# Softmax denominators from a column of ones in the value operand, with the masked scores and the exponentials sharing one double buffer

## The chip, the cores and the metric

The kernel runs on one core of one Trainium2 chip. The time is the device time of one execution in microseconds; lower is better. The core has five engines with queues of their own: PE (matmuls and weight loads), ACT (ScalarE), DVE (VectorE), POOL (GpSimd) and SP (which only starts DMAs here). Each works through its instructions in the order written, and they wait for each other through semaphores.

## The reference

For each of 32 samples (256 rows, width 384, with a 256 x 256 adjacency matrix) two graph layers are followed by a masked attention with 12 heads of width 32. The part that the change touches is the attention:

```python
scores = jnp.einsum('bhqd,bhkd->bhqk', q, k) / jnp.sqrt(32.)
scores = scores + beta * adj_e
scores = jnp.where(adj_e > 0, scores, -9e15)
probs  = jax.nn.softmax(scores, axis=-1)
out    = jnp.einsum('bhqk,bhkd->bhqd', probs, v)
x      = layernorm(x + out)
```

The graph layers ahead of it compute a softmax of h h^T times the adjacency, mix three projections of h with it, and normalise. The two layers are called a and b below.

## The kernel before

The kernel is a software pipeline over samples. In one turn of the loop, sample t is in layer a, sample t-1 in layer b, sample t-2 in the attention (stage c), and sample t-3 in the last norm and the store (stage d). The order of the steps on each engine is written out by hand in four lists, one for each of PE, ACT, DVE and POOL. A step is a word such as `scores.6`: the part of the step `scores` for head 6 that this engine does. The change leaves these lists alone. A turn with all stages takes 72.8 us.

For each head h of the attention the work goes like this; every `[P, 2, ...]` buffer is used by the parity of h:

- PE, `scores.h`: two matmuls into `bank_s`, of which there is one. It waits until DVE has read the scores of head h-1 (`s_msk`).
- DVE, `scores.h` (L852): two instructions, one for each half of the rows, that subtract the scaled scores from the bias and take the row minimum (`hmin`), into `masked`. There is one `masked` buffer, so DVE waits until ACT has read head h-1 out of it (`s_prob`).
- ACT, `scores.h` (L647): two exponentials from `masked` into `prob`, with the sum over the row taken by the instruction's accumulator into `hsum`. `prob` is double, so ACT waits until PE has transposed head h-2 (`s_pt`).
- PE, `weights.h` (L501): four transposes of `prob` into `bank_p`. It waits for the exponentials and for DVE's `weights.(h-1)`.
- ACT, `weights.h` (L654): `bank_p` to `pT_hi` (f16). DVE, `weights.h` (L858): the remainder, to `pT_lo`.
- PE, `attend.h`: eight matmuls into `bank_o`, with the high and low parts of the probabilities as weights and three or two bf16 parts of the values (`v_parts`) as the moving operand.
- DVE, `attend.h` for odd h (L868): sums the parts of two heads out of `bank_o`.

After the last head, DVE takes the reciprocal of `hsum` (`c_sum`, L876) and POOL multiplies and adds the residual (L997, L1001).

Between these steps stand the graph layers' steps. Those that the text comes to are `a_proj.0` to `a_proj.5` (ten matmuls each on PE; ACT copies the high part `hlrh`, L596, and DVE writes the remainder `hlrl`, L754; PE's `a_proj.3` waits until DVE has done `a_proj.1`, since both use the second `bank_w`), `a_turn` (PE transposes into `bank_u`, L440; DVE writes `attTl`, L759; POOL then masks four times, L956), and `b_resid`, `b_norm2`, `b_out` on DVE (L808, L811, L817 to L824), which end with `y_in`, the input of PE's `turn_y.0` (L388).

The written order on the two engines around heads 4 to 7 is

```python
# pe
... scores.6 a_proj.2 attend.3 a_turn.0 weights.4 scores.7 a_proj.3 weights.5 attend.4 scores.8 weights.6 ...
# dve
... weights.3 scores.6 a_proj.1 attend.3 weights.4 a_turn.0 scores.7 weights.5 b_resid.0 attend.4 scores.8 ...
```

Of the kernel before, what the change touches and what calls it, by code (L numbers as in the profile page):

```python
# [31 lines left out]
VP = 3  # L32
SLOTS = 3
# [59 lines left out]
def graph_attention_kernel(nc, x, adj, wl, ws, wr, bl, bs, br, ln_w, ln_b,  # L93
# [15 lines left out]
    with ExitStack() as ctx:  # L109
# [49 lines left out]
        v_parts = sb("v_parts", [P, NT, NH, VP, HD], BF16)  # L159
        v_rest = sb("v_rest", [P, NT, D])  # L160
        neg_adj = v_rest[:, :, 0:S]
        masked = sb("masked", [P, NT, S])
# [4 lines left out]
        att = result[:, :, :].rearrange("p i (h d) -> p i h d", h=NH)  # L167

        negmax = sb("negmax", [P, NT])
        ubias = sb("ubias", [P, NT])  # L170
        zsum = sb("zsum", [P, NT])
        ssum = sb("ssum", [P, NT])
        diag = sb("diag", [P, NT])
        inv_s = {k: sb(f"inv_s_{k}", [P, NT]) for k in "ab"}
        hmin = sb("hmin", [P, NT, NH])
        hsum = sb("hsum", [P, NT, NH])
# [4 lines left out]
        var = {k: sb(f"var_{k}", [P, NT]) for k in "ab"}  # L181
        var.update({k: mv[k][:, :, 1] for k in "yc"})
        eps = {"a": EPS_GRAPH, "b": EPS_GRAPH, "y": EPS_NORM, "c": EPS_NORM}
        shift = sb("shift", [P, NT])
        inv_s2 = {k: sb(f"inv_s2_{k}", [P, NT]) for k in "ab"}
        eps_col = {EPS_GRAPH: sb("eps_graph", [P, 1]), EPS_NORM: sb("eps_norm", [P, 1])}
        lnv = {k: sb(f"lnv_{k}", [P, NT]) for k in norms}
        y0 = {k: sb(f"y0_{k}", [P, NT]) for k in norms}
        tmp = {k: sb(f"tmp_{k}", [P, NT]) for k in norms}
        rstd = {k: sb(f"rstd_{k}", [P, NT]) for k in norms}  # L190
# [6 lines left out]
        staging += [y_in[:, i, :] for i in range(NT)] + [flat(masked[:, :, :])]  # L197
# [160 lines left out]
        def _(pe):  # L358
# [146 lines left out]
            def attend(t, h):  # L505
                s = t - 2
                pe.wait_ge(s_pt_lo, NH * s + h + 1)
                if h == 0:
                    pe.wait_ge(s_v_all, NT * (s + 1))
                if h % 2 == 0:  # L510
                    wait(pe, s_att, NH // 2 * s + h // 2)
                for i in range(NT):
                    at = (2 * i + h % 2) * VP * HD
                    for j in range(NT):
                        vp = v_parts[:, j, h, :, :].rearrange("p a d -> p (a d)")
                        mm(bank_o[:, at:at + VP * HD], pT_hi[:, h % 2, j, i * P:(i + 1) * P], vp, j == 0, False)
# [18 lines left out]
        def _(act):  # L535
# [98 lines left out]
            def v(t, i):  # L634
                s = t - 2
                act.wait_ge(s_v, NT * s + i + 1)
                if i == 0:
                    wait(act, s_pv, NH * s)
                nc.scalar.activation(v_parts[:, i, :, 0, :], bank_w[i][:, 0:D].rearrange("p (h d) -> p h d", h=NH),
                                     ACT.Copy).then_inc(s_v_hi, 1)  # L640
# [28 lines left out]
        def _(dve):  # L669
# [164 lines left out]
            def v(t, i):  # L834
                s = t - 2
                dve.wait_ge(s_v_hi, NT * s + i + 1)
                if i == 0:
                    dve.wait_ge(s_badj, s + 1)
                ve.tensor_tensor(v_rest[:, i, :].rearrange("p (h d) -> p h d", h=NH),
                                 bank_w[i][:, 0:D].rearrange("p (h d) -> p h d", h=NH),  # L840
                                 v_parts[:, i, :, 0, :], ALU.subtract).then_inc(s_v_rd, 1)

            def scores(t, h):
# [88 lines left out]
        def _(pool):  # L932
# [13 lines left out]
            pool.wait_ge(s_pool_c, 6)  # L946
# [44 lines left out]
            def c_sum(t, _k):  # L991
# [11 lines left out]
            def v(t, i):  # L1003
# [44 lines left out]
```

## Time and profile before

| | |
|---|---|
| median of three timed executions | 2427.14 us (2426.58 to 2428.47) |
| span of the profiled execution, first to last instruction | 2426.4 us |
| PE matmuls busy | 2020.7 us, 83% |
| DVE busy | 1771.7 us, 73% |
| ACT busy | 1289.2 us, 53% |
| POOL busy | 751.3 us, 31% |
| mean granted TensorE clock | 0.939 of full |

The timed executions have no spans of their own, so the profiled execution is known by its span alone; the median of the three times lies 0.7 us above it. The busy share of an engine is a mean over all its stages. The ends of matmuls are modelled and overlap, so a busy PE can still have room. What sets the time is read from the waits and from the chain of work that ended last.

### The profile page before, as it was taken

The numbers are of one execution on the slowest core, as the hardware profiler recorded it, in microseconds if no ns is written. First come the engines' busy times: TensorE is split into PE (matmuls) and PEld (weight loads), VectorE is DVE, ScalarE is ACT, GpSimd is POOL, SyncE is SP. The second block draws the span as 40 slices with busy tenths as digits, with TensorE's granted clock in tenths as the row PEclk, the third lists the DMA queues.
The fourth block names the chain that finished last, engine by engine and source line by source line (L and its number), as shares of the span: only waits on it lengthen the run. The fifth ranks groups of instructions, "written<-read, shape, count | busy, mean of one in ns | idle before, by whom it ended". The sixth has DMA issues, their size and how long they took to land.

```text
span 2426.4 us, 50154 instructions
## 1 busy us (share of the span) xinstructions
PE 2020.7 (83%) x14656; PEld 1882.5 (78%) x14656; DVE 1771.7 (73%) x5318; ACT 1289.2 (53%) x3612; POOL 751.3 (31%) x778
## 2 busy tenths in 40 slices
PE   4788888888888888888888888888888888888884
PEld 4788778788877788778788777788877788778773
DVE  4577777787777777777777777777777777777764
ACT  2355555555555555455555555555455555455553
POOL 0232333332333332333332333332333332333331
PEclk8999999999999999999999999999999999999975
DMA  2222222112222112222112222112222112222111
GB/s 91 63 55 73 65 67 54 48 51 71 65 67 54 48 52 71 65 67 54 49 50 71 65 67 54 48 52 71 65 67 54 47 52 71 65 67 54 42 49 45
DMA packets 144358, 144.77 MB, mean 60 GB/s; under 512 B 17596, under 2 KB 144328, under 8 KB 144328
## 3 DMA queue, kind: packets, MB, share of 16 engines
q1 hardware_dynamic: 133424, 131.20, 20.1%
q10 hardware_dynamic: 10904, 13.20, 1.6%
q8 instruction: 15, 0.25, 0.0%
q14 instruction: 15, 0.12, 0.0%
HBM read 56.25 MB, written 12.58 MB: 28 GB/s over the span
## 4 chain that ended last, share of the span: by engine, by line
PE 59%; DVE 21%; issue 11%; ACT 7%; DVEq 1%; ACTq 0%; SPq 0%; POOL 0%; DMA 0%; POOLq 0%
PE bank_w L360 27%; PE bank_m L360 9%; PE bank_u L360 6%; PE bank_p L501 6%; PE bank_s L360 3%; DVE pT_lo L858 3%; PE bank_o L360 3%; DVE masked L852 3%; ACT pT_hi L654 3%; DVE normed L808 2%; PE bank_t L377 1%; PE bank_u L440 1%; PE bank_t L388 1%; ACT hlrh L596 1%; DVE tmp_a L778 1%
## 5 line engine op out<-in xcount | busy, mean ns | idle before, releaser
L647 ACT ACTIVATE prob<-masked,hmin 128x256 f32<-128x256 f32 x768 | 383.5, 502 | 154.9 <-DVE hmin L852 153.0
L852 DVE CUSTOM_DVE_ANT_0 masked<-bank_s,bias_adj 128x256 f32<-128x256 f32 x768 | 291.8, 417 | 53.9 <-PE bank_s L360 45.1
L858 DVE TENSOR_TENSOR pT_lo<-bank_p,pT_hi 128x512 f16<-128x512 f32 x384 | 262.6, 684 | 93.2 <-ACT pT_hi L654 93.2
L654 ACT ACTIVATE pT_hi<-bank_p 128x512 f16<-128x512 f32 x384 | 228.3, 594 | 155.5 <-PE bank_p L501 147.9
L501 PE MATMUL bank_p<-ident,prob 128*128 128x128 f32 x1536 | 245.9, 284 | 77.4 <-DVE pT_lo L858 69.9
L754 DVE TENSOR_TENSOR hlrl<-bank_w,hlrh 128x384 fp32r<-128x384 f32 x256 | 139.3, 554 | 203.4 <-ACT hlrh L596 203.4
L596 ACT ACTIVATE hlrh<-bank_w 128x384 fp32r<-128x384 f32 x256 | 124.0, 485 | 291.3 <-PE bank_w L360 291.2
L501 PEld LDWEIGHTS bank_p<-ident,prob 128*128 128x128 f32 x1536 | 183.7, 145 | 101.7 <-issue 60.3
L986 POOL TENSOR_TENSOR normed<-normed,g_row 128x384 f32<-128x384 f32 x64 | 63.3, 1011 | 559.4 <-ACT normed L616 559.4
L360 PE MATMUL bank_w<-hT_ach,w_qkvh 128*128 128x256 f32 x576 | 198.4, 345 | 18.5 <-DVE qk_lo L830 12.5
L360 PE MATMUL bank_w<-w_graph0h,hT_ach 128*128 128x384 f32 x576 | 204.1, 354 | 10.5 <-DVEq L711 9.9
L360 PE MATMUL bank_w<-w_graph1h,hT_bh 128*128 128x384 f32 x576 | 208.3, 362 | 0.1
L360 PE MATMUL bank_s<-k_st,q_st 96*128 96x256 f32 x768 | 184.4, 323 | 21.0 <-issue 11.4
L360 PE MATMUL bank_w<-w_graph1h,hT_bl 128*128 128x384 f32 x576 | 199.5, 346 | 0.0
L360 PE MATMUL bank_w<-w_graph1l,hT_bh 128*128 128x384 f32 x576 | 199.5, 346 | 0.0
L360 PE MATMUL bank_w<-w_graph0l,hT_ach 128*128 128x384 f32 x576 | 195.3, 339 | 0.0
L360 PE MATMUL bank_w<-w_graph0h,hT_acl 128*128 128x384 f32 x576 | 195.2, 339 | 0.0
L360 PE MATMUL bank_w<-hT_acl,w_qkvh 128*128 128x256 f32 x576 | 180.9, 314 | 0.0
L360 PE MATMUL bank_w<-hT_ach,w_qkvl 128*128 128x256 f32 x576 | 180.8, 314 | 0.0
L360 PE MATMUL bank_o<-v_parts,pT_hi 128*128 128x96 bf16 x1536 | 169.4, 212 | 5.4 <-DVE pT_lo L858 1.2
L968 POOL TENSOR_SCALAR v_rest<-adj_in 128x512 f32<-128x512 f32 x32 | 61.7, 1927 | 350.6 <-DVE hmin L852 312.0
L956 POOL TENSOR_TENSOR uph<-attTh,mask_up 128x256 fp32r<-128x256 f32 x64 | 47.4, 740 | 372.7 <-DVE attTl L759 372.7
(200 smaller groups left out, 6236.1 us busy)
## 6 DMA issues: line engine op xcount, KB each, us to landing
x_in<-in_x SPq DMA_DIRECT2D x64, 384.0 KB, 3.3
adj_in<-in_adj SPq DMA_DIRECT2D x96, 256.0 KB, 2.8
q_st<-qk_hi SPq DMA_DIRECT2D x256, 96.0 KB, 2.2
k_st<-qk_hi SPq DMA_DIRECT2D x256, 96.0 KB, 2.2
q_st<-qk_lo SPq DMA_DIRECT2D x128, 96.0 KB, 2.2
k_st<-qk_lo SPq DMA_DIRECT2D x128, 96.0 KB, 2.2
out<-result ACTq DMA_DIRECT2D x32, 384.0 KB, 2.5
prob<-in_L_gnn_Wl SPq DMA_DIRECT2D x2, 192.0 KB, 3.6
```

The source lines that it names most:

```text
L360: return nc.tensor.matmul(dst, lhsT, rhs, start=start, stop=stop)
L501: last = nc.tensor.transpose(bank_p[:, j * S + i * P:j * S + (i + 1) * P], prob[:, h % 2, i, j * P:(j + 1) * P], ident[:, :])
L596: nc.scalar.activation(hlr[0][:, i, m // 2, :], bank_w[i][:, 0:D], ACT.Copy).then_inc(s_proj_hi, 1)
L647: nc.scalar.activation(prob[:, h % 2, i, :], masked[:, i, :], ACT.Exp, bias=hmin[:, i, h:h + 1], scale=-1.0, accum_out=hsum[:, i, h:h + 1] ...
L654: nc.scalar.activation(pT_hi[:, h % 2, :, :].rearrange("p j i -> p (j i)"), bank_p[:, :], ACT.Copy).then_inc(s_pt_hi, 1)
L754: ve.tensor_tensor(hlr[1][:, i, m // 2, :], bank_w[i][:, 0:D], hlr[0][:, i, m // 2, :], ALU.subtract).then_inc(s_proj_rd, 1)
L808: ve.scalar_tensor_tensor(normed[:, i, :], normed[:, i, :], 0.0, x_in[:, i, :], ALU.max, ALU.add).then_inc(s_resid, 1)
L852: ve.tensor_tensor_reduce(masked[:, i, :], bank_s[:, i * S:(i + 1) * S], bias_adj[:, i, :], -SCALE, BIG, ALU.add, ALU.min, hmin[:, i, h:h ...
L858: ve.tensor_tensor(pT_lo[:, h % 2, :, :].rearrange("p j i -> p (j i)"), bank_p[:, :], pT_hi[:, h % 2, :, :].rearrange("p j i -> p (j i)"), ...
L956: ins = gp.tensor_tensor(dst[part][:, :, :], blocks, keep[:, :].unsqueeze(1).to_broadcast([P, NT, P]), ALU.mult)
L968: gp.tensor_scalar(neg_adj[:, :, :], adj_in[:, :, :], 0.0, MASKED / SCALE, ALU.is_le, ALU.mult).then_inc(s_pool, 1)
L986: gp.tensor_tensor(normed[:, i, :], normed[:, i, :], g2_row[:, :], ALU.mult).then_inc(s_affine_mid, 1)
```

## The change

- The values get a 33rd column for each head and part. It is 1 in the first part and 0 in the others, so that the attention matmuls compute the sum of the exponentials as a 33rd output column. They now stream 99 and 66 columns where they streamed 96 and 64. POOL fills the column once, at the start.
- The exponentials lose their accumulator. `hsum` is gone; the reciprocal reads column 32 of the attention's sum, which goes to a tensor `att` of its own and not into `result`. POOL's multiplication reads `att` and writes `result`, and the wait for the store of the sample before stands there now.
- `masked` is gone. DVE writes into `prob[h % 2]` and ACT's exponentials work in place there. So the wait for PE's transposes of head h-2 (`s_pt`) moves from ACT's `scores.h` to DVE's `scores.h`, where it takes the place of the wait for ACT's exponentials of head h-1.
- Small two-column tensors are packed into one, `pairs`.

```diff
-        v_parts = sb("v_parts", [P, NT, NH, VP, HD], BF16)
+        v_parts = sb("v_parts", [P, NT, NH, VP, VC], BF16)
...
-        masked = sb("masked", [P, NT, S])
...
+        att = sb("att", [P, NT, NH, VC])
+
+        pairs = sb("pairs", [P, 40, NT])
...
-                    at = (2 * i + h % 2) * VP * HD
+                    at = (2 * i + h % 2) * VP * VC
...
-                        mm(bank_o[:, at:at + VP * HD], pT_hi[:, h % 2, j, i * P:(i + 1) * P], vp, j == 0, False)
-                        last = mm(bank_o[:, at:at + 2 * HD], pT_lo[:, h % 2, j, i * P:(i + 1) * P], vp[:, 0:2 * HD],
+                        mm(bank_o[:, at:at + VP * VC], pT_hi[:, h % 2, j, i * P:(i + 1) * P], vp, j == 0, False)
+                        last = mm(bank_o[:, at:at + 2 * VC], pT_lo[:, h % 2, j, i * P:(i + 1) * P], vp[:, 0:2 * VC],
...
             def scores(t, h):
                 s = t - 2
-                wait(act, s_pt, NH * s + max(h - 1, 0))
                 for i in range(NT):
                     act.wait_ge(s_msk, NT * (NH * s + h) + i + 1)
-                    nc.scalar.activation(prob[:, h % 2, i, :], masked[:, i, :], ACT.Exp, bias=hmin[:, i, h:h + 1],
-                                         scale=-1.0, accum_out=hsum[:, i, h:h + 1]).then_inc(s_prob, 1)
+                    nc.scalar.activation(prob[:, h % 2, i, :], prob[:, h % 2, i, :], ACT.Exp, bias=hmin[:, i, h:h + 1],
+                                         scale=-1.0).then_inc(s_prob, 1)
...
-                wait(dve, s_prob, NT * (NH * s + h))
+                wait(dve, s_pt, NH * s + max(h - 1, 0))
                 apart(dve)
                 for i in range(NT):
-                    ve.tensor_tensor_reduce(masked[:, i, :], bank_s[:, i * S:(i + 1) * S], bias_adj[:, i, :],
+                    ve.tensor_tensor_reduce(prob[:, h % 2, i, :], bank_s[:, i * S:(i + 1) * S], bias_adj[:, i, :],
                                             -SCALE, BIG, ALU.add, ALU.min, hmin[:, i, h:h + 1]).then_inc(s_msk, 1)
...
-                        wait(dve, s_out, 16 * s)
+                        wait(dve, s_csum_mid, NT * s)
...
-                dve.wait_ge(s_prob, NT * NH * (s + 1))
-                ve.reciprocal(hinv[:, :, :], hsum[:, :, :]).then_inc(s_hinv, 1)
+                dve.wait_ge(s_att, NH // 2 * (s + 1))
+                ve.reciprocal(hinv[:, :, :], att[:, :, :, HD]).then_inc(s_hinv, 1)
...
+            gp.memset(v_parts[:, :, :, :, :], 0.0).then_inc(s_pool_c, 1)
+            pool.wait_ge(s_pool_c, 7)
+            gp.memset(v_parts[:, :, :, 0, HD:VC], 1.0).then_inc(s_pool_c, 1)
+            pool.wait_ge(s_pool_c, 8)
...
-                pool.wait_ge(s_att, NH // 2 * (s + 1))
-                for i in range(NT):
-                    gp.tensor_tensor(att[:, i, :, :], att[:, i, :, :],
+                wait(pool, s_out, 16 * s)
+                for i in range(NT):
+                    gp.tensor_tensor(res_h[:, i, :, :], att[:, i, :, 0:HD],
```

No instruction changes its place; what changes is what some of them wait for. These are DVE's rows in the loop from `weights.3` over `scores.6` (the ISA rows) and `a_proj.1` to `attend.3`, before the change:

```order
L858 TENSOR_TENSOR pT_lo<-bank_p,pT_hi 128x512 [waits s_pt_hi]
L846 REGISTER_ALU
L246 REGISTER_ALU [waits s_sc]
L852 ISA masked,hmin<-bank_s,bias_adj 128x256 [waits s_prob]
L852 ISA hmin 128x1
L852 ISA masked,hmin<-bank_s,bias_adj 128x256
L852 ISA hmin 128x1
L753 REGISTER_ALU
L754 TENSOR_TENSOR hlrl<-bank_w,hlrh 128x384 [waits s_proj_hi]
L868 TENSOR_REDUCE result<-bank_o 128x2x64 [waits s_pv]
```

and these are the same steps of the changed kernel:

```order
L864 TENSOR_TENSOR pT_lo<-bank_p,pT_hi 128x512 [waits s_pt_hi]
L852 REGISTER_ALU
L858 ISA prob,hmin<-bank_s,bias_adj 128x256 [waits s_sc,s_pt]
L858 ISA hmin 128x1
L858 ISA prob,hmin<-bank_s,bias_adj 128x256
L858 ISA hmin 128x1
L759 REGISTER_ALU
L760 TENSOR_TENSOR hlrl<-bank_w,hlrh 128x384 [waits s_proj_hi]
L874 TENSOR_REDUCE att<-bank_o 128x2x66 [waits s_pv]
```

The wait of the masked scores is now for `s_pt`, and one of the two register instructions ahead of them is gone. `s_pt` for head 6 is counted up by the last transpose of head 4. On PE that transpose (bank_p) stands here, between `a_turn` (bank_u) and `scores.7` (bank_s) with `a_proj.3` (bank_w1) behind it; the rows are those of the changed kernel:

```order
L447 MATMUL bank_u<-ident,expu 128x128 [waits s_em]
L447 MATMUL bank_u<-ident,expu 128x128 x3
L508 MATMUL bank_p<-ident,prob 128x128 [waits s_pt_lo,s_prob]
L508 MATMUL bank_p<-ident,prob 128x128 x3
L367 MATMUL bank_s<-k_st,q_st 128x256 [waits s_msk]
L367 MATMUL bank_s<-k_st,q_st 128x256
L367 MATMUL bank_w1<-w_graph0h,hT_ach 128x384 [waits s_proj_rd]
```

PE's order and its waits are the same before and after. `scores.7` waits for DVE's `scores.6` by `s_msk`, and the first matmul of `a_proj.3` for DVE's `a_proj.1` by `s_proj_rd`; both stand on DVE behind the instruction that now waits for the transposes.

## Rows read from the trace of the kernel before

**Rows 1.** The page: span, and ACT's busy time with its instructions

```profile
span 2426.4 us, 50154 instructions
PE 2020.7 (83%) x14656; PEld 1882.5 (78%) x14656; DVE 1771.7 (73%) x5318; ACT 1289.2 (53%) x3612; POOL 751.3 (31%) x778
```

**Rows 2.** The page: the chain that ended last, share of the span by line

```profile
PE bank_w L360 27%; PE bank_m L360 9%; PE bank_u L360 6%; PE bank_p L501 6%; PE bank_s L360 3%; DVE pT_lo L858 3%; PE bank_o L360 3%; DVE masked L852 3%; ACT pT_hi L654 3%; DVE normed L808 2%; PE bank_t L377 1%; PE bank_u L440 1%; PE bank_t L388 1%; ACT hlrh L596 1%; DVE tmp_a L778 1%
```

**Rows 3.** Waits: who waited for whom, us in total, times, longest

```profile
PE bank_t L377 <- DVE normed L794: 117.4, 32, 4.0
...
PE bank_p L501 <- DVE pT_lo L858: 69.9, 74, 1.3
...
PEld bank_p L501 <- ACT prob L647: 36.4, 42, 1.3
...
DVE masked L852 <- ACT prob L647: 3.1, 6, 1.0
```

**Rows 4.** Groups by form: busy us, mean ns, idle before

```profile
L647 ACT ACTIVATION_READ_ACCUMULATOR prob<-masked,hmin 128x1 f32 x768 | 145.3, 189 | 0.0
...
L868 DVE TENSOR_REDUCE result<-bank_o 128x128 f32<-128x384 f32 x192 | 105.9, 552 | 19.8 <-PE bank_o L360 19.2
```

**Rows 5.** DVE in order of time, one turn: start, us, instruction

```profile
1020.28 0.41 DVE L852 CUSTOM_DVE_ANT_0 masked<-bank_s,bias_adj 128x256 f32<-128x256 f32 x1
...
1026.86 0.41 DVE L852 CUSTOM_DVE_ANT_0 masked<-bank_s,bias_adj 128x256 f32<-128x256 f32 x1
...
1027.54 0.08 DVE L852 DVE_READ_ACCUMULATOR2_ANT hmin<- 128x1 f32 x1
1027.54 0.55 DVE L754 TENSOR_TENSOR hlrl<-bank_w,hlrh 128x384 fp32r<-128x384 f32 x1
...
1029.69 0.68 DVE L759 TENSOR_TENSOR attTl<-bank_u,attTh 128x512 fp32r<-128x512 f32 x1
1030.29 0.41 DVE L852 CUSTOM_DVE_ANT_0 masked<-bank_s,bias_adj 128x256 f32<-128x256 f32 x1
...
1031.47 0.69 DVE L858 TENSOR_TENSOR pT_lo<-bank_p,pT_hi 128x512 f16<-128x512 f32 x1 [0.41 <-ACT pT_hi L654]
1032.08 0.68 DVE L808 SCALAR_TENSOR_TENSOR normed<-normed,x_in 128x384 f32<-128x384 f32 x1
...
1035.02 0.55 DVE L808 SCALAR_TENSOR_TENSOR normed<-normed,x_in 128x384 f32<-128x384 f32 x1
```

**Rows 6.** PE in order of time, the same turn

```profile
1019.55 0.64 PE L501 MATMUL bank_p<-ident,prob 128*128 128x128 f32 x4
...
1027.77 0.60 PE L501 MATMUL bank_p<-ident,prob 128*128 128x128 f32 x4
1028.12 0.48 PE L360 MATMUL bank_s<-k_st,q_st 96*128 96x256 f32 x2
1028.44 0.34 PE L360 MATMUL bank_w<-w_graph0h,hT_ach 128*128 128x384 f32 x1
...
1030.21 0.60 PE L501 MATMUL bank_p<-ident,prob 128*128 128x128 f32 x4
```

**Rows 7.** The last exponential of head 1 and the masked scores behind it

```profile
1013.37 0.20 ACT L647 ACTIVATION_READ_ACCUMULATOR prob<-masked,hmin 128x1 f32 x1
...
1013.75 0.42 DVE L852 CUSTOM_DVE_ANT_0 masked<-bank_s,bias_adj 128x256 f32<-128x256 f32 x1
```

**Rows 8.** The chain in order of time, one turn: start, us, what

```profile
1024.77 0.04 issue
...
1028.61 1.76 PE bank_w L360 x10
```

**Rows 9.** POOL in order of time, `a_turn` of the same turn

```profile
1031.61 0.73 POOL L956 TENSOR_TENSOR lowh<-attTh,mask_low 128x256 fp32r<-128x256 f32 x1
1032.30 1.05 POOL L956 TENSOR_TENSOR upl<-attTl,mask_up 128x256 fp32r<-128x256 f32 x1
```

**Rows 10.** A stretch at half clock: window, PE busy, granted clock

```profile
1009.70:1013.10 3.40, 3.40 (x14) 0.50 0.75 233
```

More of the change, by code:

```diff
@@ L32 @@
 VP = 3
+VC = 33
 SLOTS = 3
@@ L166, in graph_attention_kernel, with pair @@
         result = sb("result", [P, NT, D])
[L167 to L174, printed above, removed]
+        res_h = result[:, :, :].rearrange("p i (h d) -> p i h d", h=NH)
+        att = sb("att", [P, NT, NH, VC])
+        pairs = sb("pairs", [P, 40, NT])
+        places = iter(range(40))
+        def pair():
+            return pairs[:, next(places), :]
+        negmax = pair()
+        ubias = pair()
+        zsum = pair()
+        ssum = pair()
+        diag = pair()
+        inv_s = {k: pair() for k in "ab"}
         hmin = sb("hmin", [P, NT, NH])
-        hsum = sb("hsum", [P, NT, NH])
         hinv = sb("hinv", [P, NT, NH])
@@ L180, in graph_attention_kernel @@
         mv = {k: sb(f"mv_{k}", [P, NT, 2]) for k in norms}
-        var = {k: sb(f"var_{k}", [P, NT]) for k in "ab"}
+        var = {k: pair() for k in "ab"}
         var.update({k: mv[k][:, :, 1] for k in "yc"})
         eps = {"a": EPS_GRAPH, "b": EPS_GRAPH, "y": EPS_NORM, "c": EPS_NORM}
-        shift = sb("shift", [P, NT])
-        inv_s2 = {k: sb(f"inv_s2_{k}", [P, NT]) for k in "ab"}
+        shift = pair()
+        inv_s2 = {k: pair() for k in "ab"}
         eps_col = {EPS_GRAPH: sb("eps_graph", [P, 1]), EPS_NORM: sb("eps_norm", [P, 1])}
[L187 to L190, printed above, removed]
+        lnv = {k: pair() for k in norms}
+        y0 = {k: pair() for k in norms}
+        tmp = {k: pair() for k in norms}
+        rstd = {k: pair() for k in norms}
         def flat(ap):
@@ L196, in graph_attention_kernel @@
         staging = [flat(prob[:, 0, :, :]), flat(prob[:, 1, :, :]), flat(bias_adj[:, :, :])]
-        staging += [y_in[:, i, :] for i in range(NT)] + [flat(masked[:, :, :])]
+        staging += [y_in[:, i, :] for i in range(NT)] + [att[:, 0, :, :].rearrange("p h c -> p (h c)")[:, 0:D]]
         staging += [buf[:, i, :] for buf in (res, result, v_rest) for i in range(NT)]
@@ L638, in v @@
                     wait(act, s_pv, NH * s)
-                nc.scalar.activation(v_parts[:, i, :, 0, :], bank_w[i][:, 0:D].rearrange("p (h d) -> p h d", h=NH),
+                nc.scalar.activation(v_parts[:, i, :, 0, 0:HD], bank_w[i][:, 0:D].rearrange("p (h d) -> p h d", h=NH),
                                      ACT.Copy).then_inc(s_v_hi, 1)
@@ L840, in v @@
                                  bank_w[i][:, 0:D].rearrange("p (h d) -> p h d", h=NH),
-                                 v_parts[:, i, :, 0, :], ALU.subtract).then_inc(s_v_rd, 1)
+                                 v_parts[:, i, :, 0, 0:HD], ALU.subtract).then_inc(s_v_rd, 1)
             def scores(t, h):
@@ L865, in attend @@
                     if h == 1:
-                        wait(dve, s_out, 16 * s)
+                        wait(dve, s_csum_mid, NT * s)
                     dve.wait_ge(s_pv, NH * s + h + 1)
                     ve.tensor_reduce(att[:, :, h - 1:h + 1, :],
-                                     bank_o[:, 0:NT * 2 * VP * HD].rearrange("p (i h a d) -> p i h d a", i=NT, h=2, a=VP),
+                                     bank_o[:, 0:NT * 2 * VP * VC].rearrange("p (i h a d) -> p i h d a", i=NT, h=2, a=VP),
                                      AX.X, ALU.add).then_inc(s_att, 1)
@@ L945, in _ @@
                              base=0, channel_multiplier=1).then_inc(s_pool_c, 1)
-            pool.wait_ge(s_pool_c, 6)
+            gp.memset(v_parts[:, :, :, :, :], 0.0).then_inc(s_pool_c, 1)
+            pool.wait_ge(s_pool_c, 7)
+            gp.memset(v_parts[:, :, :, 0, HD:VC], 1.0).then_inc(s_pool_c, 1)
+            pool.wait_ge(s_pool_c, 8)
             pool.wait_ge(s_setup, 1)
@@ L1008, in v @@
                 rest = v_rest[:, i, :].rearrange("p (h d) -> p h d", h=NH)
-                gp.tensor_copy(v_parts[:, i, :, 1, :], rest).then_inc(s_v_mid, 1)
+                gp.tensor_copy(v_parts[:, i, :, 1, 0:HD], rest).then_inc(s_v_mid, 1)
                 pool.wait_ge(s_v_mid, NT * s + i + 1)
-                gp.tensor_tensor(v_parts[:, i, :, 2, :], rest, v_parts[:, i, :, 1, :], ALU.subtract).then_inc(s_v_all, 1)
+                gp.tensor_tensor(v_parts[:, i, :, 2, 0:HD], rest, v_parts[:, i, :, 1, 0:HD], ALU.subtract).then_inc(s_v_all, 1)
             steps = {
```

## The prediction

> **What bounds the kernel now.** I read the page first. ACT is busy for 53% of the span, PE for 83% [rows 1]. The change takes work from ACT, the second least busy of the four, so the question is whether ACT's work is on the path at all. The chain that ended last has no entry for the exponentials (L647) among its largest lines; ACT stands there with its copy pT_hi (3%) and hlrh (1%), behind PE's matmuls and several DVE lines [rows 2]. The waits say the same from the other side: DVE waited 3.1 us in the whole run for an exponential, and the weight loads of the transposes 36.4 us in total, 42 times [rows 3]. The time goes through PE, and through DVE where PE waits for it. So I look at what the change does to the order of DVE's and PE's work around one head, turn by turn.
>
> **The accumulators.** They are instructions of their own, 768 of 189 ns, 145.3 us of ACT [rows 4]. Each goes. ACT has the idle time to show for it, and nobody on the path was waiting: between nothing and 36.4 + 3.1 = 39.5 us can come back [rows 3]. Weight loads run ahead of the matmuls, so most of the 36.4 us delayed no matmul, and I take 0.
>
> **The wait that moves.** Before, DVE could write the masked scores of head h as soon as ACT had read head h-1; only ACT's exponentials had to wait until PE had transposed head h-2. Now DVE itself waits for those transposes. I compare when the masked scores of head h started with when the transposes of head h-2 ended, in one turn:
> - Head 4: started 1020.28; the transposes of head 2 ended at 1019.55 + 0.64 = 1020.19 [rows 5, 6].
> - Head 6: started 1026.86; those of head 4 ended at 1027.77 + 0.60 = 1028.37 [rows 5, 6]. It started 1.51 us too early for the new rule.
> - Head 7: started 1030.29; those of head 5 ended at 1030.21 + 0.60 = 1030.81 [rows 5, 6]. 0.52 us too early.
>
> The other heads have their transposes done 0.3 us or more ahead. The turns repeat, so this holds in each.
>
> From the release to the start of the masked scores there is the semaphore instruction between them: the exponential of head 1 ended at 1013.37 + 0.20 = 1013.57 and the masked scores of head 2, which had waited for it, started at 1013.75, so 0.18 us [rows 7].
>
> Now the turn again with the new rule. DVE is in order, so what stands behind the masked scores waits too: `a_proj.1`, `attend.3`, `weights.4`, `a_turn`. On PE `scores.7` waits for the masked scores of head 6, and `a_proj.3` for `a_proj.1`.
> 1. Masked scores of head 6: 1028.37 + 0.18 = 1028.55, 1.69 later. They end with the last read of the minimum, which stood at 1027.54 + 0.08 = 1027.62, 0.76 after the start [rows 5]: now 1029.31.
> 2. PE goes on about 0.06 after such a read (0.04 of issue [rows 8]): `scores.7` at 1029.37, before 1028.12 [rows 6]: 1.25 later. PE stands still here.
> 3. `a_proj.1` follows 0.68 after the start of the masked scores and takes 0.55 [rows 5]: 1029.23 to 1029.78. So `a_proj.3` starts at 1029.84, before 1028.44 [rows 6]: 1.40 later. This step is a piece of the chain [rows 8], so nothing takes the delay up.
> 4. The transposes of head 5 come directly behind it: 1031.61, ended 1032.21. Masked scores of head 7: 1032.39. Behind them on DVE stands pT_lo of head 5, 0.68 later at 1033.07; before, it started at 1031.47 [rows 5]: 1.60 later. pT_hi would have been ready 0.2 us sooner, so the masked scores now hold it.
> 5. PE's next transposes wait for that pT_lo, and on DVE `b_resid` follows it at once (1032.08 [rows 5]), with the whole chain to `y_in` behind it. Head 8's transposes and masked scores shift by the same amount. 1.60 us goes on into the next turn.
>
> Small terms of the same place: head 4 has to wait until 1020.19 + 0.18 = 1020.37, 0.09 later than before. Against it, one of the two register instructions ahead of each masked scores goes; where DVE's sequencer sets the pace, that gives something of the same size back (an estimate, between 0 and 0.1 us, since no row shows the instruction alone). I let them cancel.
>
> There are 30 turns with layer a beside the attention: 30 x 1.60 = 48.0 us. The two last samples run beside less or no graph work, the wait bites there too but with PE less full; I take 1.5 us each, 3.0, and 0 to 6 as its bounds.
>
> **The wider matmuls.** Five columns in 160 more, 3.1%. At most the whole of this comes on the chain's share of bank_o, 3% of 2426.4 or 73 us [rows 1, 2]: 2.3 us, taken whole. The bound above it is that the odd start of the columns (99 elements of 2 bytes) slows the reading; that is a rival below. **DVE's sum** grows from 384 to 396 elements: at most 12/384 of 552 ns, 17 ns, 192 times [rows 4], 3.3 us, of which about one in six lies on the path: 0.5 us. **The fills** of the value column run once on POOL while the weights are still being loaded and split, and nobody waits for POOL then; uncovered they would cost a few us, I take 0. The reciprocal, POOL's multiplication of as many elements, the moved wait for the store (a turn old by then) and the packed pairs: 0.
>
> **Sum.** 48.0 + 3.0 + 2.3 + 0.5 = 53.8 us on the profiled span of 2426.4: 2480.2. The median of the runs is 0.7 above that span: 2481 us.
>
> **Rival: the port.** DVE's L808 took 0.68 us at 1032.08 and 0.55 at 1035.02 when POOL had finished, and POOL's third mask took 1.05 where its neighbour took 0.73 [rows 5, 9]: the two engines hold each other up. DVE's `a_turn` step (L759) comes behind the shifted `a_proj.1`, the sum of head 3 and pT_lo of head 4: 1029.78 + 0.55 + 0.69 + 0.68 less the 0.2 by which they overlap is 1031.5, where it ended at 1029.69 + 0.68 = 1030.37 before [rows 4, 5]. POOL's four masks of 0.7 us each come behind it, so the last one starts near 1033.7, just when the shifted L808 starts (1033.68). If POOL comes first, L808 waits for the mask's 0.73 us; if DVE comes first, it gains the 0.13 that it lost before. The cost is -4 to +22 us over 30 turns. The case in which POOL comes first gives 2481 + 22 = 2503 us. The Trainium skill (SBUF — State Buffer, "SBUF: two separate sides") says that a DVE instruction with two SBUF inputs and a GpSimd instruction that reads SBUF take an exclusive lock for a whole instruction, whichever starts first; by that rule, what I call holding up is a full block, and the trace agrees with it here.
>
> **Rival: the clock.** PE now stands still for about 1.3 us at 1028.5 and 1.2 us more around 1032.6. The trace has stretches with the granted clock at 0.50, that is 1.2 GHz in place of 2.4 [rows 10], each of about 3.4 us; PE's longest wait, 4.0 us for L794, stands once in each turn [rows 3]. If the new pauses bring one more per turn, it costs up to 1.7 us of PE work, of which DVE's chain to `y_in` hides about half: 30 x 0.85 = 25 us, 2506 us. Against it: pauses of up to 1.3 us for pT_lo stand in each turn already [rows 3].
>
> **Rival: faster.** If the exponentials were what the transposes wait for, and the weight loads' waits were real, removing the accumulators would give back 36.4 + 3.1 us, and with the wait hidden the time would be 2427 - 39 = 2388 us, a little more with the wider matmuls. It decides if head 6's masked scores start no earlier than their transposes end; they start 1.5 us earlier [rows 5, 6].
>
> **Rival: nothing.** PE idles up to 4.0 us later in the turn [rows 3]; if that idle took the delay up, 3 us of wider matmuls would be left: 2430 us. Against it: that idle ends with DVE, and the chain runs through the delayed pieces.
>
> **Rival: slow reading.** If bf16 columns that start off a 4-byte boundary (odd heads) streamed at half speed, half of the 73 us would double: 2481 + 37 = 2518 us. No row shows such an operand.
>
> **How the numbers follow.** A measurement of this kernel can tell about 0.2% (5 us) from no change. Chances: the forecast 0.50 (2465 to 2495), the port 0.20, the clock 0.12, slow reading 0.04, nothing 0.05, faster 0.05, something else 0.04. The range reaches from a wait half a microsecond a turn cheaper with some return from ACT (2481 - 15 - 10 = 2456) over the port and the clock to a little beyond (2515). Faster 0.05, same 0.05, slower 0.90.
>
> **What would show it.** Of the changed kernel: DVE's masked scores of heads 6 and 7 idle before they start, with PE's transposes (bank_p) as the releaser, about 1 us and 0.6 us per turn; PE idle before bank_s and bank_w in the same places, released by DVE's hmin and hlrl; a turn of about 74.5 us in place of 72.8; no accumulator rows on ACT, about 145 us less busy; the spacing of bank_o's matmuls a few per cent up. I am wrong if DVE's idle is there and the turn is not longer (then there was slack that I did not see), if the turn is much longer with the granted clock at 0.50 in more stretches than one or two a turn, or if L808 takes over 1 us.

## The result and the profile after

The changed kernel takes 2501.1 us (median of four, 2498.1 to 2502.4) against 2427.8 us (2426.6 to 2428.8) for the kernel before on the same chip: a ratio of 1.030, 95% interval 1.029 to 1.031. That is 73 us more, where the prediction had 54. The profiled execution spans 69.9 us more than that of before. The page of the changed kernel, to be read against [rows 1, 2]:

```profile
span 2496.3 us, 48977 instructions
PE 2058.6 (82%) x14656; PEld 1901.7 (76%) x14656; DVE 1782.0 (71%) x5318; ACT 1228.8 (49%) x2844; POOL 743.4 (30%) x780
...
PE bank_w L367 29%; PE bank_m L367 9%; PE bank_u L367 6%; PE bank_p L508 6%; PE bank_s L367 4%; DVE prob L858 4%; DVE pT_lo L864 3%; PE bank_o L367 3%; DVE normed L814 2%; ACT pT_hi L660 2%; DVE normed L800 1%; PE bank_u L447 1%; PE bank_t L384 1%; DVE pairs L785 1%; PE bank_t L395 1%
```

ACT does its exponentials in 768 instructions fewer and is busy 60 us less, where the prediction expected some 145 us less. DVE is busy 10 us more, in a span that is 70 us longer. The masked scores (now `prob`, L858) have gone from 3% to 4% of the chain. The waits, against [rows 3]; columns: who waited for whom, us in total, times, longest:

```profile
PE bank_t L384 <- DVE normed L800: 113.5, 32, 4.0
...
PE bank_s L367 <- DVE hmin L858: 61.5, 71, 1.8
...
DVE prob L858 <- PE bank_p L508: 57.5, 37, 1.9
...
PE bank_p L508 <- DVE pT_lo L864: 50.8, 70, 1.3
...
DVE prob L858 <- issue: 32.3, 31, 1.6
...
PEld bank_p L508 <- ACT prob L653: 27.5, 71, 1.3
```

DVE waits for the transposes 37 times, 57.5 us; behind it PE waits 71 times, 61.5 us, for the minima. The row with "issue", once a turn, is head 7: the transposes of head 5 had been issued and ended (1060.98) while DVE stood there. One turn in order of time, DVE first. Times are compared from the start of head 0's masked scores: 1035.67 here, and in the turn of [rows 5] of the kernel before 1007.02 (second fence). 28.65 us lie between.

```profile
1035.67 0.41 DVE L858 CUSTOM_DVE_ANT_0 prob<-bank_s,bias_adj 128x256 f32<-128x256 f32 x1
...
1057.21 0.42 DVE L858 CUSTOM_DVE_ANT_0 prob<-bank_s,bias_adj 128x256 f32<-128x256 f32 x1 [1.62 <-PE bank_p L508]
...
1061.15 0.42 DVE L858 CUSTOM_DVE_ANT_0 prob<-bank_s,bias_adj 128x256 f32<-128x256 f32 x1 [1.02 <-issue]
...
1061.85 0.69 DVE L864 TENSOR_TENSOR pT_lo<-bank_p,pT_hi 128x512 f16<-128x512 f32 x1
1062.45 1.04 DVE L814 SCALAR_TENSOR_TENSOR normed<-normed,x_in 128x384 f32<-128x384 f32 x1
...
1065.76 0.55 DVE L814 SCALAR_TENSOR_TENSOR normed<-normed,x_in 128x384 f32<-128x384 f32 x1
```

```profile
1007.02 0.41 DVE L852 CUSTOM_DVE_ANT_0 masked<-bank_s,bias_adj 128x256 f32<-128x256 f32 x1
```

PE and POOL in the same turn of the changed kernel:

```profile
1056.43 0.60 PE L508 MATMUL bank_p<-ident,prob 128*128 128x128 f32 x4
1058.04 0.50 PE L367 MATMUL bank_s<-k_st,q_st 96*128 96x256 f32 x2 [1.01 <-DVE hmin L858]
1058.51 0.45 PE L367 MATMUL bank_w<-w_graph0h,hT_ach 128*128 128x384 f32 x1
...
1060.38 0.60 PE L508 MATMUL bank_p<-ident,prob 128*128 128x128 f32 x4
...
1061.99 0.50 PE L367 MATMUL bank_s<-k_st,q_st 96*128 96x256 f32 x2 [0.71 <-DVE hmin L858]
```

```profile
1062.35 0.72 POOL L965 TENSOR_TENSOR lowl<-attTl,mask_low 128x256 fp32r<-128x256 f32 x1
```

Each start less 28.65 and less its start in [rows 5, 6]:

| step | forecast | measured |
|---|---|---|
| masked scores of head 6 | 1.69 | 1057.21 - 28.65 - 1026.86 = 1.70 |
| scores.7 | 1.25 | 1058.04 - 28.65 - 1028.12 = 1.27 |
| a_proj.3 | 1.40 | 1058.51 - 28.65 - 1028.44 = 1.42 |
| pT_lo of head 5 | 1.60 | 1061.85 - 28.65 - 1031.47 = 1.73 |
| first L814 (L808 before) | 1.60 | 1062.45 - 28.65 - 1032.08 = 1.72 |
| second L814 | 1.60 | 1065.76 - 28.65 - 1035.02 = 2.09 |

The transposes of head 4 ended at 1057.03, and the masked scores of head 6 started 0.18 behind them. Up to the first L814 the forecast is within 0.13 us of the trace; 0.10 of the 0.13 comes in between `a_proj.3` and the transposes behind it (1058.51 to 1060.38, 1.87 us, where it was 1.77). Between the two L814 another 0.37 comes in: the first took 1.04 us where it took 0.68 [rows 5]. POOL's fourth mask started at 1062.35, 0.10 ahead of this L814, and ended at 1063.07.

The wider instructions, against [rows 4] (552 ns for the sum); mean ns behind the busy time:

```profile
L814 DVE SCALAR_TENSOR_TENSOR normed<-normed,x_in 128x384 f32<-128x384 f32 x64 | 50.5, 789 | 0.8 <-POOL normed L998 0.8
...
L367 PE MATMUL bank_o<-v_parts,pT_hi 128*128 128x99 bf16 x1536 | 173.8, 213 | 5.2 <-DVE att L874 0.9 <-DVE pT_lo L864 0.9
...
L874 DVE TENSOR_REDUCE att<-bank_o 128x132 f32<-128x396 f32 x192 | 108.5, 565 | 20.6 <-PE bank_o L367 20.3 <-issue 0.3
```

A matmul with 99 columns takes 213 ns (212 with 96), DVE's sum 13 ns more than before.

From head 0's masked scores to the next sample's, a steady turn (mean of 26, from sample 3 on) takes 75.02 us, before 72.85: 2.17 more.

### The profile page after: what moved, and what is told of

It is laid out like the page before. It is cut to its first block, busy times and chain, and to the rows that moved or that the text cites. A ratio compares the mean times of both kernels' runs of the same rounds, so it can differ in the third digit from the quotient of the medians.

```text
span 2496.3 us, 48977 instructions
## 1 busy us (share of the span) xinstructions
PE 2058.6 (82%) x14656; PEld 1901.7 (76%) x14656; DVE 1782.0 (71%) x5318; ACT 1228.8 (49%) x2844; POOL 743.4 (30%) x780
## 4 chain that ended last, share of the span: by engine, by line
PE 61%; DVE 22%; issue 11%; ACT 5%; DVEq 1%; ACTq 0%; SPq 0%; POOL 0%; DMA 0%; POOLq 0%
PE bank_w L367 29%; PE bank_m L367 9%; PE bank_u L367 6%; PE bank_p L508 6%; PE bank_s L367 4%; DVE prob L858 4%; DVE pT_lo L864 3%; PE bank_o L367 3%; DVE normed L814 2%; ACT pT_hi L660 2%; DVE normed L800 1%; PE bank_u L447 1%; PE bank_t L384 1%; DVE pairs L785 1%; PE bank_t L395 1%
## 5 line engine op out<-in xcount | busy, mean ns | idle before, releaser
L653 ACT ACTIVATE prob<-prob,hmin 128x256 f32<-128x256 f32 x768 | 348.8, 502 | 169.1 <-DVE hmin L858 168.2
L858 DVE CUSTOM_DVE_ANT_0 prob<-bank_s,bias_adj 128x256 f32<-128x256 f32 x768 | 292.9, 419 | 138.3 <-PE bank_p L508 57.5
L508 PE MATMUL bank_p<-ident,prob 128*128 128x128 f32 x1536 | 253.9, 291 | 59.0 <-DVE pT_lo L864 50.8
L367 PE MATMUL bank_s<-k_st,q_st 96*128 96x256 f32 x768 | 183.7, 322 | 74.2 <-DVE hmin L858 61.5
L367 PE MATMUL bank_w<-w_graph1h,hT_bh 128*128 128x384 f32 x576 | 219.8, 382 | 0.1
L367 PE MATMUL bank_w<-w_graph1l,hT_bh 128*128 128x384 f32 x576 | 209.0, 363 | 0.0
L367 PE MATMUL bank_w<-w_graph1h,hT_bl 128*128 128x384 f32 x576 | 207.3, 360 | 0.0
L367 PEld LDWEIGHTS bank_s<-k_st,q_st 96*128 96x128 f32 x768 | 128.2, 197 | 92.8 <-DVE hmin L858 81.0
L367 PE MATMUL bank_o<-v_parts,pT_hi 128*128 128x99 bf16 x1536 | 173.8, 213 | 5.2 <-DVE att L874 0.9
```

The costliest lines, as they stand in the source:

```text
L367: return nc.tensor.matmul(dst, lhsT, rhs, start=start, stop=stop)
L508: last = nc.tensor.transpose(bank_p[:, j * S + i * P:j * S + (i + 1) * P], prob[:, h % 2, i, j * P:(j + 1) * P], ident[:, :])
L653: nc.scalar.activation(prob[:, h % 2, i, :], prob[:, h % 2, i, :], ACT.Exp, bias=hmin[:, i, h:h + 1], scale=-1.0).then_inc(s_prob, 1)
L858: ve.tensor_tensor_reduce(prob[:, h % 2, i, :], bank_s[:, i * S:(i + 1) * S], bias_adj[:, i, :], -SCALE, BIG, ALU.add, ALU.min, hmin[:, i, ...
```

## The experiments

Ratios are to the kernel before on the same chip, with 95% intervals. "Half-clock time" is what the record of the granted clock shows at 0.50 (1.2 GHz) between 220 and 2150 us, for each turn: 5.94 us in the kernel before, 6.90 in the changed one (6.30 and 6.69 over the 26 steady turns alone). It comes in stretches of 3.4 us or twice that.

`e2`, `e3`, `e4`, `e6` and `e11` need room for one more buffer. They leave out the loads of the rows `v_bias` and `b2_row` and add `g2_row` in their place: the same additions, with other values, and two loads fewer at the start.

### The moved wait alone, and the rest without it

`e1_inplace_only`, on the kernel before; accumulators and 32 columns stay:

```diff
 # ACT, scores.h
-wait(act, s_pt, NH * s + max(h - 1, 0))
-nc.scalar.activation(prob[:, h % 2, i, :], masked[:, i, :], ACT.Exp, ...
+nc.scalar.activation(prob[:, h % 2, i, :], prob[:, h % 2, i, :], ACT.Exp, ...
 # DVE, scores.h
-wait(dve, s_prob, NT * (NH * s + h))
+wait(dve, s_pt, NH * s + max(h - 1, 0))
-ve.tensor_tensor_reduce(masked[:, i, :], ...
+ve.tensor_tensor_reduce(prob[:, h % 2, i, :], ...
```

> The kernel before with only the buffers changed: DVE writes the masked scores into prob, the exponentials work in place and keep their accumulators, and the wait for the transposes stands on DVE. Values stay 32 wide. Theory (the moved wait alone costs the time): about 72 us slower than before, 2496 to 2502 us, with DVE idle before the masked scores of heads 6 and 7 and a turn of about 75.1 us. Rival (the wider matmuls or the new sum cost a good part): at least 15 us less, under 2485 us.

Measured: 2501.06 us, 1.030 (1.028 to 1.031), the time of the changed kernel to 0.1 us. Its waits:

```profile
PE bank_s L360 <- DVE hmin L851: 62.2, 71, 1.8
...
DVE prob L851 <- PE bank_p L501: 57.8, 37, 1.9
```

`e2_ones_only` is the reverse of this diff on the changed kernel (column of ones, no accumulators, a separate `masked`, the old waits):

> The changed kernel with a separate masked buffer and the waits of before; the column of ones, no accumulators. To make room, the rows v_bias and b2_row are not loaded and g2_row stands for both, so two additions use other values. Theory: within 6 us of before (2424 to 2433 us): the wider matmuls cost about 2 us, the accumulators give back almost nothing. Rival (wide or odd columns are slow): 2440 us or more. Rival (accumulators were on the path): under 2415 us.

Measured: 2427.58 us, 1.000 (0.999 to 1.001). In the profiled execution head 0's first masked scores start 1.9 us earlier than in the kernel before (133.75 against 135.61), so up to 2 us of wider matmuls could hide there.

`e3_ones_acc` is e2 with the accumulators run for nothing:

```diff
-    scale=-1.0).then_inc(s_prob, 1)
+    scale=-1.0, accum_out=hsum[:, i, h:h + 1]).then_inc(s_prob, 1)
```

> As the kernel with the column of ones and a separate masked buffer (g2_row stands for v_bias and b2_row here too), but the exponentials also run their accumulators into a tensor that nobody reads. Against that kernel it prices the accumulators, against before the wider matmuls. Theory: 0 to 3 us above it, since ACT is off the path. Rival (ACT matters): 10 us or more above it.

Measured: 2428.53 us, 1.000 (0.999 to 1.001).

`e4_triple` is the changed kernel, in place, with a third buffer (`h % 3` wherever `prob` is indexed; shown are the other two lines) and the wait one head looser:

```diff
-prob = sb("prob", [P, 2, NT, S])
+prob = sb("prob", [P, 3, NT, S])
-wait(dve, s_pt, NH * s + max(h - 1, 0))
+wait(dve, s_pt, NH * s + max(h - 2, 0))
```

> The changed kernel with three prob buffers in place of two, so that DVE waits for the transposes of head h-3 (g2_row stands for v_bias and b2_row, for room). Every such wait is over before DVE comes to it. Theory: all of the loss comes back, 2424 to 2433 us, a turn of about 72.8 us. Rival (the loss is in the column, or in the exponentials in place): it stays at 2490 us or more.

Measured: 2427.56 us, 0.999 (0.998 to 1.000).

So the whole difference is DVE's wait for the transposes of head h-2. The accumulators, 145.3 us in their rows [rows 4], are worth nothing that can be measured here (e2 against e3: 1 us), and neither are the wider matmuls and their odd starts. Their 145.3 us were never all ACT's to give back: ACT is busy 1218.8 us in e2 and 1290.3 in e3, 71.5 apart. Each accumulator's row overlaps the exponential ahead of it and the one behind it, as in the kernel before:

```profile
1025.29 0.51 ACT L647 ACTIVATE prob<-masked,hmin 128x256 f32<-128x256 f32 x1
1025.69 0.20 ACT L647 ACTIVATION_READ_ACCUMULATOR prob<-masked,hmin 128x1 f32 x1
1025.79 0.50 ACT L647 ACTIVATE prob<-masked,hmin 128x256 f32<-128x256 f32 x1
```

### Which head, and the order of PE

`e6_head6` is e4 with the tight wait put back at head 6 alone:

```diff
-wait(dve, s_pt, NH * s + max(h - 2, 0))
+wait(dve, s_pt, NH * s + (h - 1 if h == 6 else max(h - 2, 0)))
```

> The kernel with three prob buffers (g2_row stands for v_bias and b2_row), in which DVE waits for the transposes of head h-2 at head 6 alone. Theory, by the steps of the prediction: the masked scores of head 6 start 1.7 us later, a_proj.3 1.4 us, and pT_lo of head 5 then only 1.4 in place of 1.6: 1.4 us a turn and the port's 0 to 0.4 on top, 2468 to 2485 us. Rival (head 7's wait or both together matter): under 2455 us.

Measured: 2485.62 us, 1.023 (1.021 to 1.025), just above the expected span. Head 11 starts 1.47 us later in a turn, two thirds of the 2.16 of the full change. But the half-clock time of the profiled execution, the longest of the four, is 8.76 us a turn, and its steady turn takes 75.07 us, no less than that of the changed kernel. That the stretches took the difference is likely, but not shown.

`e7_early_w4` lets PE of the changed kernel do the transposes of head 4 before `attend.3` and `a_turn.0`:

```diff
-a_proj.2 attend.3 a_turn.0 weights.4 scores.7 a_proj.3 weights.5 ...
+a_proj.2 weights.4 attend.3 a_turn.0 scores.7 a_proj.3 weights.5 ...
```

> The changed kernel with one step moved in PE's list: weights.4 directly behind a_proj.2, ahead of attend.3 and a_turn.0. Head 4's transposes then end about 0.84 us sooner. Theory: masked scores of head 6 start 0.85 us later than before the change in place of 1.69, and the turn gets 0.8 us longer in place of 2.3: 2448 to 2468 us. Rival (the loss doesn't come from when these transposes end): 2490 us or more.

Measured: 2470.77 us, 1.018 (1.017 to 1.020): 30 us of the loss back, 3 us short of the expected span. DVE's wait for the transposes fell from 57.5 to 38.0 us. Head 11 starts 0.99 us later in a turn than before the change, in place of 2.16.

### The port

`e5_held_mask` makes POOL's fourth mask wait until the first L814 is done, on the changed kernel:

```diff
 for dst, keep in ((up, mask_up), (low, mask_low)):
+    if held is not None and part == 1 and dst is low:
+        wait(pool, s_resid, held)
     ins = gp.tensor_tensor(dst[part][:, :, :], blocks, ...
```

> The changed kernel, and POOL's fourth mask of a_turn waits until DVE's first b_resid is done, so that the two no longer meet. In the changed kernel that b_resid takes 1.04 us where it needs 0.55. Theory (the port rival came in): b_resid back at 0.55 and about 0.4 us less a turn, 2485 to 2492 us. Rival (the meeting is covered, or the clock's stretches take the gain): 2497 us or more.

Measured: 2493.8 us (2487.3 to 2496.5), 1.026 (1.025 to 1.028): 7 us less than the changed kernel where 9 to 16 were expected, 1.8 us above the expected span. The meeting itself is gone. L814 in e5, against 789 ns above:

```profile
L814 DVE SCALAR_TENSOR_TENSOR normed<-normed,x_in 128x384 f32<-128x384 f32 x64 | 35.8, 559 | 0.8 <-POOL normed L1000 0.8
```

0.23 us on 64 instructions is 14.7 us of DVE. In the profiled execution the turn is 74.99 us, as long as without this edit (75.02), and the half-clock time rose from 6.90 to 7.96 us a turn.

DVE and POOL meet at a second place, in both kernels: DVE's step `h_apply` (four small instructions, then L794, which writes the `normed` that PE transposes) stands beside POOL's `c_sum` and its addition into `res` (L978). `e8_before_held_sum` is the kernel before with POOL's `c_sum` held until DVE has done them:

```diff
 pool.wait_ge(s_hinv, s + 1)
+pool.wait_ge(s_h1, NT * (t if not isinstance(t, int) or t <= NB else NB))
```

> The kernel before, and POOL's c_sum also waits until DVE's h_apply is done. In the trace of before, h_apply's five DVE instructions end one after the other with POOL's, 1052.6 to 1057.9, and PE waits 4.0 us for them, in each turn. Theory (they hold each other up through the shared port): h_apply ends about 3 us sooner and the turn is 2 to 3.4 us shorter, 2330 to 2370 us. Rival (POOL's work, begun later, comes late for the last norm or the values): no gain or a loss, 2425 us or more.

Measured: 2295.67 us, 0.945 (0.944 to 0.947), 133 us faster and far past the expected span. L794 of the kernel before and of e8:

```profile
L794 DVE TENSOR_SCALAR normed<-mixed,mv_a,rstd_a 128x384 f32<-128x384 f32 x64 | 76.8, 1239 | 1.2
```

```profile
L794 DVE TENSOR_SCALAR normed<-mixed,mv_a,rstd_a 128x384 f32<-128x384 f32 x64 | 27.8, 477 | 1.2
```

PE's waits in e8:

```profile
PE bank_t L377 <- DVE hT_bl L724: 42.2, 34, 1.7
...
PE bank_t L377 <- DVE normed L794: 5.2, 2, 4.0
```

PE's wait for L794, once a turn and 117.4 us [rows 3], is down to 5.2 us. It isn't all gained: PE now waits at the same place for `hT_bl`, which it hardly did before (6.6 us, 11 times), so that the pause shrinks from 3.8 to 1.3 us. How the two engines met in the kernel before, DVE first:

```profile
1054.44 0.92 DVE L779 SCALAR_TENSOR_TENSOR rstd_a<-tmp_a,rstd_a 128x2 f32<-128x2 f32 x1
1055.39 2.11 DVE L794 TENSOR_SCALAR normed<-mixed,mv_a,rstd_a 128x384 f32<-128x384 f32 x1
```

```profile
1054.35 0.99 POOL L1001 TENSOR_TENSOR result<-result,res 128x384 f32<-128x384 f32 x1
1055.49 1.80 POOL L978 TENSOR_TENSOR res<-y_in,v_bias 128x768 f32<-128x768 f32 x1
```

DVE's instructions end 0.02 and 0.2 us behind POOL's. The Trainium skill (SBUF — State Buffer, "SBUF: two separate sides") says that a GpSimd instruction and a DVE instruction that runs in a two-port mode, or that has two SBUF inputs while the GpSimd instruction reads SBUF, block each other for whole instructions, and that the one that starts first goes ahead. These rows and the 1239 against 477 ns agree with the blocking. They don't show who wins: L794 is recorded as started 0.10 us ahead of L978 and still ended behind it, and no row tells in which mode L794 runs.

The turn went from 72.85 to 68.25 us, and the half-clock time from 5.94 to 0.48 us: most of the stretches had stood behind the pause of 3.8 us on PE (next part).

### The moved wait where the clock is nearly undisturbed

`e9_after_held_sum` is the same hold on the changed kernel:

> The changed kernel with POOL's c_sum held until h_apply is done, as in the kernel before with the same hold (2295.7 us), which has hardly any stretch at half clock left. It prices the change where the clock takes no part. Theory: the moved wait 1.65 us and the meeting of b_resid with POOL's mask 0.36 us a turn, 2.0 us, and some 5 us outside the full turns and in the wider matmuls: 2350 to 2366 us. Rival (the clock's stretches were a large part of the loss): under 2345 us; or PE's new pauses bring stretches back: over 2370 us.

Measured: 2398.82 us, 0.987 (0.986 to 0.989), a miss. Here the change costs 103 us against e8. The half-clock time is 3.55 us a turn: a stretch stands in each turn behind PE's pause for `hT_acl`, and in e8, where this pause is as long, in 4 of 26 turns. PE at that pause in e9, and the stretch (window, busy times by engine, then the granted clock):

```profile
1067.74 0.69 PE L374 MATMUL bank_t<-ident,x_in 128*128 128x128 f32 x2 [2.11 <-DVE hT_acl L721]
```

```profile
1067.59:1071.00 3.41, 3.26 (x13) 3.26 (x14) 1.68 (x7) 1.71 (x4) 0.42 (x1) 0.50 0.60 210
```

So the pause itself had to be shortened. `e10_before_held_two` is e8 with POOL's masks of layer b held until DVE has done `c_apply`:

```diff
 pool.wait_ge(s_at_lo, n + 1)
+if held is not None:
+    pool.wait_ge(s_out_ok, held)
```

> The kernel before with c_sum held until h_apply is done, and POOL's masks of b_turn held until c_apply is done. In the trace of before c_apply's two instructions take 0.84 us each where 0.48 would do, and two small ones ahead of them 0.7 us where 0.16 would do, while POOL does the masks of b_turn; PE's turn_x.2 waits 2.1 us behind them. Theory: about 1.7 us less a turn than with c_sum held alone, 2240 to 2265 us. Rival (the masks come late for b_mix, or the values for attend.0): 2290 us or more.

Measured: 2270.81 us, 0.935 (0.933 to 0.936), short of the expected gain over e8 but the fastest kernel here that computes the reference in full.

`e11_ones_held_two` is e2 with both holds:

> The column of ones without accumulators and with a separate masked buffer (g2_row stands for v_bias and b2_row), and both holds of POOL's work. It asks whether the freed ACT time is worth something once the turn is shorter. Theory: still off the path, within 6 us of the kernel with both holds and the accumulators. Rival (ACT comes onto the path in the shorter turn): 10 us or more faster than it.

Measured: 2259.07 us, 0.932 (0.929 to 0.935), 12 us below e10 and so outside the expected 6, where the rival has it. But the traces don't bear the rival out. A turn without a stretch takes 67.09 us here (24 of the 26) and 67.16 in e10 (20 of 26), so the accumulators and the column are worth at most 0.07 us a turn, some 2 us. Of the 13.5 us between the two profiled executions 2.6 lie ahead of the first sample's masked scores, and most of the rest in the turns in which e10 has a stretch and e11 has none (half-clock time 0.95 against 0.24 us a turn).

`e12_after_held_two` is the changed kernel with both holds:

> The changed kernel with both holds on POOL, against the kernel before with the same two holds (2270.8 us). The question is what the moved wait costs where hardly any stretch at half clock is left around it. Direct delay alone (1.65 us a turn up to pT_lo of head 5, some 2.0 to 2.2 with the meeting on the port): 30 turns give 50 to 65 us and the last samples 3 to 5, so 2323 to 2341 us, a turn of 69.1 to 69.7 us and half-clock time under 1.5 us a turn. Rival: the pause at head 6 brings the stretches back, as it did under the first hold, where the change cost 103 us: 2365 us or more, with half-clock time of 3 us a turn or more. Between the two, both have a share in proportion to the half-clock time.

Measured: 2331.1 us, 0.960 (0.959 to 0.962), in the middle of the expected span: 60.3 us above e10. The turn is 69.51 us, 2.07 longer than in e10, at 0.74 us of half-clock time; turns without a stretch, 20 of 26 in both, take 69.25 and 67.16, 2.09 apart. DVE's wait is the same as without the holds, and PE's pauses at heads 6 and 7 too:

```profile
DVE prob L858 <- PE bank_p L508: 57.5, 37, 1.9
```

```profile
1059.16 0.51 PE L367 MATMUL bank_s<-k_st,q_st 96*128 96x256 f32 x2 [1.01 <-DVE hmin L858]
...
1063.10 0.50 PE L367 MATMUL bank_s<-k_st,q_st 96*128 96x256 f32 x2 [0.71 <-DVE hmin L858]
```

```profile
1040.00:1109.00 69.00, 60.57 (x459) 55.67 (x457) 50.55 (x165) 37.64 (x89) 22.76 (x24) 1.00 0.23 63
```

The last fence is nearly a whole turn of e12 at a granted clock of 1.00. The new pauses of 1.0 and 0.7 us have no stretch behind them in any turn. An old one has, though: in 6 turns of 26, here as in e10, a stretch stands behind PE's pause of 1.3 us for `pT_lo`. One of them in e12:

```profile
661.85 0.82 PE L508 MATMUL bank_p<-ident,prob 128*128 128x128 f32 x3 [1.28 <-DVE pT_lo L864]
```

```profile
661.90:665.30 3.40, 3.40 (x23) 3.31 (x24) 0.96 (x2) 0.98 (x2) 2.17 (x2) 0.50 0.00 0
```

## Why the prediction was right, and where its sizes were off

**Where the time fell.** 2501 us lies inside the stated range, but outside the forecast's own 2465 to 2495 us, and 2 us from the figure of the port rival (2503, chance 0.20). That nearness is luck: the meeting at the port came in at half its price, and the rest came from other terms. The wait that moves, with 48 of the 54 us forecast, is the cause.

**The accumulators, taken at 0.** Right: e3 runs them for nothing and is 1 us slower, within the noise. PE's matmuls themselves waited for exponentials 1.3 us in the whole run; the 36.4 us [rows 3] are weight loads' waits:

```profile
PE bank_p L501 <- ACT prob L647: 1.3, 2, 1.0
```

The sign "about 145 us less busy" didn't come, because the rows of the accumulators overlap their neighbours: 60 us.

**The wait that moves.** Right, and shown to be the whole change by e1 on one side and e2 and e4 on the other. Its steps up to the first `b_resid` stand in the trace within 0.13 us. What DVE and PE idle there was not as forecast: DVE 1.62 and 1.02 us (about 1 and 0.6), PE 1.01 and 0.71 (1.3 and 1.2).

**1.60 us a turn.** This is the term that was too small. The delay of 1.60 up to pT_lo of head 5 is 1.71 (median over turns with the same stretches), but at head 11 it is 2.16, and the steady turn is 2.17 longer. 30 x 2.17 = 65.1 in place of 48.0. The step that failed is "`b_resid` follows it at once ... with the whole chain to `y_in` behind it. ... 1.60 us goes on into the next turn": L814 met POOL's fourth mask. The rival had the place to 0.1 us (mask near 1033.7, that is 1062.35 less 28.65), and POOL did come first. Its price of 0.73 was too high: 0.37 of it was added. Its sign, L808 over 1 us, is there (1.04). e5, which keeps the two apart, has 559 ns for L814 and heads 8 to 11 some 0.5 us earlier in a turn. Of the 0.57 us that 2.17 has over 1.60, 0.13 stand at pT_lo of head 5, 0.36 at the second L814, and the last 0.1 I have not traced to a step.

**The clock rival** did not come in as I put it. PE's pauses of 1.01 and 0.71 us at heads 6 and 7 have no stretch behind them, here or in e12. In the changed kernel the stretches of the steady turns stand behind the same two pauses as before, of 2.1 us for `hT_acl` and up to 3.8 us for L800 (L794 before). The first pause has one in 25 of 26 turns, before in 12; behind the second it lasts 3.4 us in every turn, where before it lasted 6.8 us in 10 of 26. One turn:

```profile
1036.83 0.44 PE L374 MATMUL bank_t<-ident,x_in 128*128 128x128 f32 x2 [2.11 <-DVE hT_acl L721]
```

```profile
1037.59:1041.00 3.41, 3.41 (x14) 3.41 (x13) 1.58 (x6) 0.70 (x2) 0.00 (x0) 0.50 0.98 304
1058.04:1061.45 3.41, 3.23 (x24) 2.87 (x24) 2.39 (x5) 0.98 (x3) 2.59 (x4) 1.00 0.00 0
```

The second window is the one behind the pause at head 6: granted clock 1.00. The two shifts nearly cancel in the steady turns (6.30 and 6.69 us at half clock), and turns that have 3.4 us behind each pause take 72.8 us before (3 turns) and 75.1 now (25), 2.3 apart: the steady 2.17 is not the clock's. In the second turn it is different: from 209 to 287 us, the changed kernel has 13.7 us at half clock and that of before 3.4, and this turn alone is 5.85 us longer, 3.7 more than a steady one. One of its stretches stands behind the pause of 1.3 us for `pT_lo`, so "pauses of up to 1.3 us for pT_lo stand in each turn already" was no argument against new ones. Over the whole span, a mean clock of 0.939 in both is 297 and 305 us at half clock.

**The last two samples, 3.0.** They cost 0.2: from head 0's masked scores of the one to those of the other takes 0.26 us less than before, from there to the end 0.45 more. The wait delays the very last sample's head 11 by 0.75 us, of which the end keeps 0.45. **The wider matmuls, 2.3, and DVE's sum, 0.5.** Nothing to be measured: e2 is 0.8 us below the kernel before, and e1, which has neither, takes as long as the changed kernel. The matmuls took 213 and 197 ns, where they took 212 and 196; "a few per cent" was too much.

**The sum as measured:** the 30 turns with layer a cost 69.6 us, that is 65.1 for the steady 2.17, 3.7 for the second turn and 0.8 for the others' departures. With 0.2 ahead of the first turn and 0.2 for the last two samples this is 69.9, up to rounding. The median of the runs is 73.3 above. The other three executions of the changed kernel span 2498.2 to 2500.7 us at a mean clock of 0.935 to 0.936, the profiled one 2496.3 at 0.939; what they had more is not in any trace.

**The other rivals.** "Nothing" falls with e1. "Faster" falls with e2 and e3. "Slow reading": 213 against 212 ns. What remains open is how much of the 73 us belongs to the clock. With it almost out of play the change costs 60.3 us (e12 against e10), so about 13 us may be the clock's, if the holds on POOL change nothing else; under one hold the change cost 43 us more than that (e9 against e8).

## What to carry to other kernels

When a buffer is dropped, list for each head the time between the old start of its writer and the end of its last reader: two negative gaps (1.5 and 0.5 us) in a turn of 73 us decided this case, and a third buffer (e4) undid it at once. Work removed from an engine that nobody waits for (60 us of ACT's busy time here) is worth nothing, and it can't pay for one wait on the engine that others follow. Before moving waits, look for DVE instructions far above their usual duration beside POOL work with slack: one wait instruction on POOL was worth 5.5% (e8).

## What the runs showed of the hardware that I had not expected

- DVE instructions of two elements a partition took 0.8 to 0.9 us beside POOL's work where the same ones took 0.15 to 0.16 in e8 (one of the three, kernel before; another, L779, is shown above):

```profile
1052.62 0.81 DVE L776 TENSOR_TENSOR rstd_a<-y_a,inv_s_a 128x2 f32<-128x2 f32 x1
```

- A saved pause can be worth more than its length. e8 shortened DVE's work by some 3.6 us a turn and PE's pause by 2.5, and the turn by 4.6: nearly all of the half-clock time, 5.5 us a turn, went with it. A saved wait can also be worth less: e5 took 0.23 us off each L814 and left the turn as long as it was, with 1.1 us more at half clock.
- Which pause gets a stretch was not settled: nearly the same pause of 2.1 us had one in each turn of e9 and in 4 turns of 26 of e8, and one of 1.3 us had one in 6 turns of 26 of e10 and e12.
